# Second cross attention: TensorE takes a step's last scores and its third turn of context ahead of the turn of the next batch's maxima

## The reference, cut to what matters

```
xn = layernorm(x, gm, bm)                 # context of the batch, 1601 x 128
ln = layernorm(latents, gl, bl)           # 64 x 128
q = ln @ Wq
kv_input = jnp.concatenate([xn, ln], axis=-2)
k, v = jnp.split(kv_input @ Wkv, 2, axis=-1)
sim = jnp.einsum('bhid,bhjd->bhij', heads(q) / scale, heads(k))
sim = sim - max(sim, axis=-1)
attn = jax.nn.softmax(sim, axis=-1)
out = (attn @ v) @ Wout
```

## Time and profile before

| | us |
|---|---|
| median of 3 runs | 3098.39 (3097.78 to 3103.08) |
| span of the profiled execution, first to last instruction | 3101.7 |
| TensorE busy | 2838.7 (92%) |
| VectorE busy | 1989.4 (64%) |
| GpSimd busy | 1906.1 (61%) |
| ScalarE busy | 1480.4 (48%) |

### The profile page before, as it was taken

How to read it: one execution, slowest core, us unless ns; L and a number is a source line. 1 busy time by engine, 2 the same in 40 slices (tenths; PEclk the granted TensorE clock), 3 DMA queues, 4 the chain that set the end, 5 groups by cost and what they waited for, 6 DMA issues and landing times. The chain is left out here.

```text
span 3101.7 us, 67025 instructions
## 1 busy us (share of the span) xinstructions
PE 2838.7 (92%) x22782; PEld 1632.0 (53%) x22829; DVE 1989.4 (64%) x4520; ACT 1480.4 (48%) x2387; POOL 1906.1 (61%) x1278
## 2 busy tenths in 40 slices
PE   5799999999999978998899999999999997887789
PEld 2355555555555566775344444444444443777356
DVE  5477777777777754114567767767767744776653
ACT  3466666666666622333544444444444434223633
POOL 5487878787878821001488888888888871553500
PEclk8799999999999988998999999999999998999789
DMA  6655555555555201001000000000000000000300
GB/s 182 185 175 194 175 192 178 192 177 189 181 187 174 91 3 56 0 0 38 22 32 21 21 32 21 21 32 21 21 32 21 21 1 9 3 3 12 75 4 10
DMA packets 148252, 233.13 MB, mean 75 GB/s; under 512 B 16788, under 2 KB 85852, under 8 KB 148125
## 3 DMA queue, kind: packets, MB, share of 16 engines
q1 hardware_dynamic: 146972, 228.87, 22.6%
q10 hardware_dynamic: 1152, 2.49, 0.6%
HBM read 147.80 MB, written 83.52 MB: 75 GB/s over the span
## 5 line engine op out<-in xcount | busy, mean ns | idle before, releaser
L444 POOL TENSOR_TENSOR sb_a_acc<-sb_a_acc,sb_a_PT 128x1024 f32<-128x1024 f32 x252 | 596.5, 2367 | 37.1 <-ACT sb_a_PT L522 30.8
L522 ACT ACTIVATE sb_a_PT<-ps_a_SC 128x1024 f32<-128x1024 f32 (+1 forms) x416 | 425.8, 1023 | 315.1 <-PE ps_a_SC L794 288.6
L607 DVE TENSOR_REDUCE sb_a_mx<-ps_a_A 128x1 f32<-128x512 f32 x768 | 506.6, 686 | 97.0 <-PE ps_a_A L771 91.7
L1692 POOL TENSOR_TENSOR sb_a_acc<-sb_a_acc,sb_a_PT 128x512 f32<-128x512 f32 (+2 forms) x384 | 487.6, 1270 | 37.3 <-ACT sb_a_PT L1788 10.9
L1788 ACT ACTIVATE sb_a_PT<-ps_a_SC 128x1024 f32<-128x1024 f32 (+2 forms) x256 | 234.3, 916 | 564.1 <-PE ps_a_SC L2067 330.5
L2086 PE MATMUL ps_a_PV<-sb_a_PT,sb_a_XN 128*128 128x512 f32 (+2 forms) x896 | 435.4, 602 | 2.2 <-ACT sb_a_PT L1788 0.7
L1881 DVE TENSOR_REDUCE sb_a_mx<-ps_a_A 128x1 f32<-128x512 f32 x384 | 256.7, 679 | 279.6 <-PE ps_a_A L2042 240.0
L2067 PE MATMUL ps_a_SC<-sb_a_QX,sb_a_XT 128*128 128x512 f32 (+1 forms) x832 | 396.7, 596 | 0.1
L771 PE MATMUL ps_a_A<-sb_a_KS,sb_a_QS 97*128 97x512 bf16 x768 | 301.9, 394 | 29.8 <-issue 17.3
L794 PE MATMUL ps_a_SC<-sb_a_QS,sb_a_KS 105*128 105x128 bf16 (+1 forms) x3328 | 257.7, 220 | 13.4 <-DVE sb_a_QS L621 13.4
L805 PE MATMUL ps_a_PV<-sb_a_PT,sb_a_V 128*32 128x256 f32 (+1 forms) x3328 | 266.7, 392 | 0.4 <-issue 0.3
(11 more groups left out here) (521 smaller groups left out, 5317.3 us busy)
## 6 DMA issues: line engine op xcount, KB each, us to landing
sb_a_C<-in_ctx_dram SPq DMA_DIRECT2D x64, 768.0 KB
a_KD<-sb_a_K SPq DMA_DIRECT2D x192, 256.0 KB, 4.1
sb_a_KS<-a_KD SPq DMA_DIRECT2D x256, 192.0 KB
a_KD<-sb_a_K SPq DMA_DIRECT2D x192, 144.2 KB, 2.7
sb_a_KS<-a_KD SPq DMA_DIRECT2D x256, 108.2 KB
sb_a_QP<-a_QD ACTq DMA_DIRECT2D x6, 384.0 KB, 15.0
sb_a_dn<-n_L_ffn_expert_down_dram SPq DMA_DIRECT2D x1, 2048.0 KB, 15.2
a_QD<-sb_a_PT SPq DMA_DIRECT2D x3, 384.0 KB, 6.0
```

What stands on the lines that cost most here:

```text
L444: pool.tensor_tensor(acc[:, :], first[:, :], PT[slot(a, j)][:, :], ALU.add).then_inc(s["acc"], 1)
L522: act.activation(PT[slot(a, j)][0:n, :], SC[(a + j) % 2][0:n, :], ACT.Exp).then_inc(s["exp"], 1)
L607: v.tensor_reduce(mx[:, p, c:c + 1], A[u % 2][:, :], AXX, ALU.max).then_inc(s["am"], 1)
L1692: pool.tensor_tensor(acc[a][0:m, :], first, PT[u % 4][0:m, HQ * i:HQ * i + HQ], ALU.add).then_inc(s["acc"], 1)
```

## The change

Two statements of TensorE's `step` move, the turn of the maxima `top(b + 1)` and the rotation `rotate(b + 2)`, both in u = 6. Nothing is added or taken away, and no other engine's list changes.

```diff
                 for u in range(NB):
                     us = units(u) if one else ()
-                    if u == 6 and one:
-                        top(b + 1)
                     if u + 1 < NB:
                         scores(b, a, u + 1)
...
                     if u == 2 and old:
                         total(b - 1, 1 - a)
+                    if two and u in turns(b):
+                        turn(b + 2, a, turns(b)[u], pair if a == 0 and old else None)
+                    if u == 6 and one:
+                        top(b + 1)
                     if u == 6 and two:
                         rotate(b + 2)
-                    if two and u in turns(b):
-                        turn(b + 2, a, turns(b)[u], pair if a == 0 and old else None)
                     if u == 5 and old and a == 0:
                         out(b - 1, not two)
```

## The result

| | before | after |
|---|---|---|
| median of the runs | 3098.09 us (4 runs) | 3216.50 us (4 runs, 3215.53 to 3218.74) |
| ratio, 95% interval | 1 | 1.038 (1.0366 to 1.0395) |
| span of the profiled execution | 3101.7 us | 3214.0 us |

A forecast was written before the change was run, and what follows sets the result against it. TensorE, busy 92%, was taken to bound the kernel through its order and waits. Odd steps 14 x (-1.48 + 6.25 + 2.5) = +101.8, with +2.9, -3.4 and -3: +98, 3197 us; range 3130 to 3225.

The forecast's parts named there:

- Top's wait goes: TensorE, odd steps: last scores and third turn fill top's 1.48 us wait for the maxima, 14 times, -20.7 us.
- costed at 0.1: Each of 29 steps: ScalarE's copy of the third turn comes later and delays the fourth turn 0.1 us, +2.9 us.
- Gain earlier, norm not: Odd steps: gain(b + 2) begins at 2115.21 instead of 2116.59, while norm(b + 3), held by GpSimd's additions, still ends at 2116.69.
- Five tiles, 6.25 us of wait: Odd steps: gain and shift hold norm's five remaining tiles, copy_out is late, and products(b + 1, 0) wait 6.25 us.
- the chain: Odd steps: gain, then shift hold norm's tiles until shift's end, copy_out follows at 2123.3, and products(b + 1, 0) wait.
- The clock, 2.5 us: Behind each new wait in odd steps, slow clock costs 2.5 us, with ends 1.7 and 3.0.
- Even steps: Norm's last tile starts with 0.3 us to spare ahead of gain: no collision and no cost.
- the rival: Even steps collide as well: norm's last tile held by gain, products wait 1.7 us more, 14 times; 3221 us, chance 0.10.
- The small gains: Half clock behind two of top's waits goes, -3.4 us, and the first step's wait is filled with work, -3 us.
- The two slow stretches of before: Behind two of top's 14 waits the clock is 0.50 for 3.4 us; both taken as gone, -3.4 us.
- The first step: Last scores and third turn, at full then half clock, fit into top's 3.79 us wait there, -3 us.

The follow-up runs named there:

- Experiments 1 and 3: 1: the change, with gain(b + 1) also waiting for norm(b + 2), 3080.88 us; 3: kernel before with only the last scores moved ahead of top, 3244.43 us.
- the third kernel: Against the kernel before, top alone moves, between the last scores and rotate; the turns stay where they were: 3244.43 us, ratio 1.0463.
- the first experiment: Against the change, GpSimd's gain(b + 1) also waits for VectorE's norm(b + 2): 3080.88 us, ratio to before 0.9937.
- The early-maxima kernel: Against the kernel before, TensorE's order kept, VectorE's addition of epsilon made by GpSimd ahead of power: 3217.93 us, ratio 1.038.
- the cut-up kernel: Against the change, the long instruction of gain and of shift cut into six of two tiles each: 3108.47 us, ratio 1.0023 to before.

## Why the prediction was right, and what it missed

**Top's wait goes.** Right: two of 16 are left. The gain of an odd step was 1.18 us rather than 1.38, and an even step, costed at 0.1, takes 0.30 more. From products(b, 5) to products(b + 1, 0), odd: 2119.13 - 2106.24 = 12.89 before. After, that place is 2178.14: top at 2170.24 and the 7.90 us from there that an even step of after needs (2138.52 to 2146.42 on the timeline). That makes 11.71, and an even step, which took 11.41 before (2074.82 to 2086.23), takes as long. Of the 0.30, 0.15 lie between the third turn and top, 0.59 us (2169.65 to 2170.24) instead of the turn's 0.44; 0.09 are the fourth turn's wait for ScalarE (forecast 0.1); 0.06 come later.

**Gain earlier, norm not.** Right in kind and place: gain starts 9.17 us behind products(b, 5), 10.35 before. Experiments 1 and 3 confirm that this decides.

**Five tiles, 6.25 us of wait.** The count of tiles was right, the wait came out as 7.53 (2178.14 to 2185.67). Missed was the last term of the chain. I ended the collision with shift's short instruction, but GpSimd's list goes on, and the fifth tile was held through the next one too, the addition at 2183.63, 1.25 us long.

**The clock, 2.5 us.** A pair of steps went from 66.19 us (tops at 2076.71 and 2142.90) to 75.09 (2138.52 to 2213.61), by 8.90. Less 7.53 for the wait, and with 1.18 - 0.30 = 0.88 for the gain, 2.25 are left for the clock. The forecast's 2.5 was chosen between 1.7 and 3.0, from waits of 1.43 and 3.79 us; that it came so near is partly luck. This is the usual pair: the first five grew by less, the very first by 8.17 us, and the last by 10.4, since its odd step had no wait for maxima before; over the 14 this cancels.

**Even steps.** Right: there is 0.34 us between norm's end and gain, forecast 0.3. How near the rival was the third kernel shows.

**The small gains.** The two slow stretches of before are gone (3.4 us): two pairs there took 67.88 us for the others' 66.2, and no pair of after stands out so. The first step, from its top to the next one, is 3.97 us shorter for a forecast of 3, and that is luck. In the kernel before the clock was 0.50 for 6.4 us behind the first top, in the profiled execution of after it was 1.00. In the first experiment, with the same order of TensorE, it was 0.50 for 6.6 us there, and its first step is only 1.13 us shorter than before's. So some 2.8 of the 3.97 us are the clock of that one execution, which the forecast, with its 1.77 us of work put into the wait, had not reckoned with.

The sum: 14 x 8.90 - 3.4 - 4.0 - 0.2 for the last step = +117.0, which is what the stretches show. The forecast's +98 lacks 14 x 1.28 = 18 us of wait, and 14 x 0.4 us for the slower order (0.2 in each odd step, 0.2 more than forecast in each even one); the clock gives 14 x 0.25 = 3.5 back. The first and the last step came out 1.2 us better. The addition's hold is nearly all of the miss.

## What to carry to other kernels

Before you fill a regular wait of the busiest engine, ask what starts when it moves forward: here a buffer's release let a GpSimd instruction of 3.44 us start beside VectorE tiles that follow one another every 0.26 us, and one tile for each such instruction paid its whole length. Where the instruction that comes too early has time to spare, let it wait for the short ones (the wait cost nothing in the kernel before and turned +118 us into -19), or cut it up, so that a hold is as long as a piece. And count a chain of holds to the end of the other engine's list, not to the end of the instruction that began it.

## What the runs showed of the hardware

- A norm tile recorded 0.07 us **ahead** of gain (2175.53 and 2175.60) was held for all of gain, just as one 0.08 us behind it (2161.32 and 2161.24). So a start in the profile doesn't tell which of two came first at this distance.
- In the change's odd step one tile got through at each boundary between two GpSimd instructions but one: the last tile didn't pass between shift's short instruction and the addition behind it, 1.76 us for a tile that takes 0.33 when it isn't held. The early-maxima kernel shows the same 1.76.
- A wait of 7.58 us left 4.3 us of half clock behind it, at a price of some 2.2 us. Fourteen waits of 1.6 us in the cut-up kernel left the clock of its steps at 1.00; behind two of the waits of 1.43 us in the kernel before it had been 0.50. What tells these apart, no run here shows.
- The order of unlike matmuls on TensorE isn't free: the third turn (float32) between the last scores and top (bfloat16) costs 0.15 us more than behind rotate. Only that place was seen.
